# Edge sum of a two-layer graph network: a step's sum is added six steps behind its mark on VectorE instead of four

## The chip, the cores and the metric

The kernel runs on one core of a Trainium2 chip. The metric is the device time of one execution in microseconds (us); smaller is better. The kernel before takes 4176.44 us (median of three runs, 4168.92 to 4176.94).

## The reference

There are 12,500 nodes with 64 features each and 400,000 edges, sorted by their destination node. Every edge has a source, a destination and 64 attributes of its own. Two layers follow each other; cut to what matters:

```python
# layer 0
agg  = segment_sum(x[src], dst)
mean = agg / maximum(deg, 1)
h = relu(concat([x, mean]) @ W_fc + b_fc) + x @ W_res + b_res
x = layernorm(x + h)
# layer 1, two convolutions (the second on relu of the first)
msg = x[src] @ Wm + bm + edge_attr @ We + be
out = segment_sum(msg, dst) + x @ Ws + bs
x = layernorm(x + out)
```

Since `edge_attr @ We` is linear, its sum over the edges of a node is the sum of the edge attributes of that node, times `We`. The kernel therefore sums the attributes once, before either convolution needs them. This **edge sum** is the stage that the change touches: for each node, the sum of `edge_attr` over the edges that end in it.

## The kernel before, in words

The program has a preparing part (index tables, about 310 us), then three rounds of gathering and summing over the source nodes (`r` = 0, 1, 2), and between rounds 0 and 1 the edge sum. Each engine has a stream of its own, written out by hand, and streams meet at semaphores only. No scheduler orders anything: the order on each engine is the order of the code.

**A step of the edge sum.** The edges are cut into 625 groups of 640 (`EG` = 5 tiles of 128 edges). The nodes are cut into 98 blocks of 128. A step is one group with one block that its edges may end in; there are 728 steps (`ESTEPS`), which run in 91 passes of a loop with eight steps each (`EB` = 8). Which group and which block a step has is read from tables made earlier: `path` (groups) and `steps` (block numbers, one byte each, four to a word, lines 436 to 444). `h` is the step's place in the pass, 0 to 7, and also the number of its buffers: everything of a step lies in the `h`-th of eight slots, and its sum in PSUM bank `h`.

For each step:

- **SyncE (SP, lines 1498 to 1504)** loads the 160 KB of attributes of the group into `feats[h]`, once TensorE has finished with the slot (`e_mm[h]`). Before the first of the eight loads of a pass it reads eight group numbers from `path` into registers (line 431).
- **GpSimd (POOL, lines 1239 to 1248)** subtracts the first node of the block from the destinations of the group: `rel_e[h]`.
- **VectorE (DVE, line 878)** compares this with the numbers 0 to 127 and so makes the **mark** of the step, `mark_e[h]`: for each of the 640 edges a row of 128 places with a one at its node.
- **ScalarE (ACT, line 1373)** copies the marks of two steps at once from fp16 to fp32 (`hot_e`).
- **TensorE (PE, line 1130)** multiplies attributes and marks: five matrix products per step, recorded as ten, alternating between the two halves of the partitions of bank `h`. The last one raises `e_mm[h]`.
- **VectorE (line 889)** adds bank `h` to `sums_e` of the step's block: the **addition** of the step. It raises `e_add`, on which TensorE waits before it writes a bank again (line 1127).

**The order on VectorE** is what the change touches. In place `h` of the loop it makes the mark of step `h` and then the addition of the step that lies `LAG` = 4 behind (line 885: `b = (h - LAG) % EB`). In the first pass the first four additions add banks that were set to zero (line 871). After the loop four additions are left over (lines 890 to 895). Then TensorE folds the two halves together (lines 1135 to 1141), and round 1 begins.

```python
bs = load_blocks(i * (EB // 4) + (SETS * GW + GW - LAG) // 4, EB)
...
b = (h - LAG) % EB
dve.wait_ge(e_mm[b], i + (2 if h >= LAG else 1))
dve.wait_ge(e_add, i * EB + (h + EB))
to = flat(sums_e[:, bass.ds(bs[h], 1), :])
V.tensor_tensor(to, to, ps[:, b, 0:P], ALU.add).then_inc(e_add, 1)
```

Of the kernel before, what the change touches and what calls it, by code (L numbers as in the profile page):

```python
# [29 lines left out]
U8 = mybir.dt.uint8  # L30
# [5 lines left out]
P = 128  # L36
# [52 lines left out]
def gnn_program(nc, step_c, x, src, dst, edge_attr, W_fc, b_fc, W_res, b_res,  # L89
# [10 lines left out]
    D0, D1 = B0 * P, END * P  # L100
    REG, (RUNS, CSTEPS) = regions(), runs()
    BACK = max(k for _, _, _, k, _ in RUNS)
    CG = -(-CSTEPS // P)
    HIS = BLOCKS
    WIN = HIS * WD
    HALF = HIS // 2
    G, GW = 6, 8
    GI = WITH
    SG = -(-(T + BLOCKS - 1) // P)
    SPAD = SG * P  # L110
# [4 lines left out]
    EG = 5  # L115
    GROUPS = T // EG
    EB = 8
    LAG = 4
    ESTEPS = -(-(GROUPS + BLOCKS - 1) // EB) * EB
    ES = -(-(ESTEPS + 1) // P)  # L120
    NB = 7
# [8 lines left out]
    CH = 512 // VC  # L130
    CW = CG * P
    spans_of = [(s0, (REG + [(0, 0, 0, 0, CW)])[n + 1][4], wd) for n, (_, _, wd, _, s0) in enumerate(REG)]
    PIECES = 16
    HB, RING = 4, 16
# [6 lines left out]
    SETS = SPAD // G  # L141
    STEPS = SETS * GW + ES * P
# [4 lines left out]
    assert 3 * CG >= 64 and 4 * CG >= BLOCKS  # L147
    assert UNION >= YW >= BLOCKS * D and G * F1 <= 512 and 0 < GI <= ITERS and all(b <= 2 * GI or b - n >= 2 * GI for n, b in ((r[1], r[0] + r[1]) for r in REG)) and B0 >= 0 and DB % 2 == 0 and WPB % HB == 0
    assert all(n % 2 == 0 and s0 % P == 0 and sum(d) * WD // wd % RING == 0 for _, n, wd, ds, s0 in REG for d in ds) and HIS % 2 == 0 and (SETS - SETS % 2) * G >= T + BLOCKS - 1

    ctx = ExitStack()
    with ctx:
        def sb(name, shape, dt=F32):
            return ctx.enter_context(nc.sbuf_tensor(name, shape, dt))

        def sem(name):
            return ctx.enter_context(nc.semaphore(name))
# [13 lines left out]
        steps_dram = nc.dram_tensor("steps_dram", [SPAD + ES * P], U8).ap()  # L171
# [10 lines left out]
        code_g = sb("code_g", [P, SPAD], F16)  # L182
        src_g = sb("src_g", [P, SPAD], I16)
        path = sb("path", [1, PATH], I16)
        steps = sb("steps", [1, GW + STEPS], U8)
        base_e = sb("base_e", [P, ES * P])
        rel_e = sb("rel_e", [P, EB, EG, 2], F16)
        ident = sb("ident", [P, P])
# [68 lines left out]
        def c_ps(b):  # L257
            return ps[:, b, 0:CH * VC].rearrange("p (g v) -> p g v", v=VC)
# [54 lines left out]
        s_zero = sem("s_zero")  # L313
# [13 lines left out]
        s_path_in = sem("s_path_in")  # L327
# [108 lines left out]
        def load_blocks(frm, n):  # L436

            words = steps[0:1, :].bitcast(I32)
            _, packed = nc.values_load_multi_w_load_instructions(  # L439
                words[0:1, bass.ds(frm, n // 4)], engines=(ENG.DVE,), min_val=0,  # L440
                max_val=(BLOCKS - 1) * 0x01010101,
                skip_runtime_bounds_check_because="four block numbers, each clamped when the path was made")
            return [nc.s_assert_within(b, 0, BLOCKS - 1, skip_runtime_bounds_check_because="one of the four block numbers")
                    for v in packed for b in (v & 0x7F, (v >> 8) & 0x7F, (v >> 16) & 0x7F, v >> 24)]

        def flat(v):
            return v.rearrange("p b d -> p (b d)")
# [3 lines left out]
        def _(dve):  # L451
            V = nc.vector
            count = [0]

            def step(ins, name=None):

                count[0] += 1
                ins.then_inc(s_v, 1)
                dve.wait_ge(s_v, count[0])
                if name:  # L460
                    mark[name] = count[0]

            V.memset(steps[0:1, 0:GW + SETS * GW], 0).then_inc(s_zero, 1)
            V.memset(w_cat[:, :, :, :], 0.0).then_inc(s_zero, 1)
            V.memset(w_y0[:, :, :], 0.0).then_inc(s_zero, 1)
            dve.sem_inc(e_add, EB)
# [42 lines left out]
            for b in range(-(-CG // CH)):  # L509
                cols = slice(b * CH, min(b * CH + CH, CG))  # L510
                n = cols.stop - cols.start
                at, last = c_ps(b)[:, 0:n, :], found_c[:, 0:n, :]
# [174 lines left out]
            for r in range(3):  # L687
# [82 lines left out]
                if r == 0:  # L770
# [5 lines left out]
                    for b0, blocks, wd, deeps, s0 in REG:  # L776
                        upto, pair = steps_upto(wd, deeps)
                        many = at_once(wd)
                        with dve.Fori(0, blocks // 2) as i:
                            for j in range(2):  # L780
# [3 lines left out]
                                for q in range(upto[j][0], upto[j][WPB]):  # L784
# [12 lines left out]
                                    if part == 0:  # L797
                                        dve.wait_ge(b_used[j], it + (1 + j))
                                        if b0 < 2 * GI:
                                            bs = load_blocks((it * 2 + j) * (GW // 4), GW)  # L800
# [69 lines left out]

                step(V.memset(ps[:, EB - LAG:EB, 0:P], 0.0), "zeros_e")
                with dve.Fori(0, ESTEPS // EB) as i:
                    bs = load_blocks(i * (EB // 4) + (SETS * GW + GW - LAG) // 4, EB)
                    for h in range(EB):
                        if h % 2 == 0:
                            dve.wait_ge(e_hot[h // 2], i + 1)
                        dve.wait_ge(e_rel[h], i + 1)
                        marks = V.tensor_tensor(mark_e[:, h, :, :].rearrange("p j (c u) -> p j c u", u=2),  # L878
                                                lane16[:, 0:P].rearrange("p (c u) -> p c u", u=2).unsqueeze(1)
                                                .to_broadcast([P, EG, P // 2, 2]),  # L880
                                                rel_e[:, h, :, :].unsqueeze(2).to_broadcast([P, EG, P // 2, 2]),
                                                ALU.is_equal)
                        if h % 2:
                            marks.then_inc(e_mark[h // 2], 1)
                        b = (h - LAG) % EB
                        dve.wait_ge(e_mm[b], i + (2 if h >= LAG else 1))
                        dve.wait_ge(e_add, i * EB + (h + EB))
                        to = flat(sums_e[:, bass.ds(bs[h], 1), :])
                        V.tensor_tensor(to, to, ps[:, b, 0:P], ALU.add).then_inc(e_add, 1)  # L889
                last = load_blocks((SETS * GW + ESTEPS + GW - LAG) // 4, LAG)  # L890
                for k in range(LAG):
                    dve.wait_ge(e_mm[EB - LAG + k], ESTEPS // EB + 1)
                    dve.wait_ge(e_add, ESTEPS + k + EB)
# [491 lines left out]
        def _(sp):  # L1385
# [6 lines left out]
            row = lambda a: a.rearrange("(a n) -> a n", a=1)  # L1392
# [37 lines left out]
            for frm, to, cols in ((32, 0, ES), (56, PATH - P, 1)):  # L1430
# [4 lines left out]
            sp.dma_start(path[:, :], row(path_dram)).then_inc(s_path_in, 16)  # L1435
            sp.dma_start(steps[:, GW:GW + SETS * GW].rearrange("a (s e) -> a s e", e=GW)[:, :, 0:G],
                         row(steps_dram[0:SETS * G]).rearrange("a (s e) -> a s e", e=G)).then_inc(s_path_in, 16)
            sp.dma_start(steps[:, GW + SETS * GW:GW + STEPS], row(steps_dram[SPAD:SPAD + ES * P])).then_inc(s_path_in, 16)
            sp.dma_start(base_e[:, :], row(base_dram).to_broadcast([P, ES * P])).then_inc(s_path_in, 16)
            for r in range(3):  # L1440
                if r:
# [105 lines left out]
```

## Time and profile before

| what | before |
|---|---|
| median of three runs | 4176.44 us |
| lowest, highest | 4168.92, 4176.94 us |
| span of the profiled execution (first to last instruction) | 4128.3 us |
| mean granted TensorE clock over the span | 0.941 of full speed |
| PE busy over the span | 3373.4 us, 82% |
| VectorE, ScalarE, GpSimd busy | 57%, 40%, 48% |
| edge sum: first mark to last addition of the loop | 1594.9 to 2230.9 us |
| its last addition, after the loop | starts at 2234.21 us |
| fold of the halves on PE | 2234.55 to about 2256.5 us |

The times are read like this. A run's time is that of the whole execution; the span of the profiled execution is the part from its first to its last instruction, and 48.1 us lie between that span and the median of the runs. The profile gives no run time of its own for the profiled execution, so its span stands for it. The edge sum takes about 15% of the span, in one stretch, in which only the lines named above work. Register, semaphore and DMA-issuing instructions do not count as busy, so SyncE has no busy time at all in the profile; what it does shows in the starts of its DMAs and in the rows of its queue (SPq).

### The profile page before, as it was taken

Reading aid. Unit: us, or ns where it says so; the run is one execution under the profiler, and the core shown is the slowest. Engines: PE = TensorE matmul, PEld = TensorE weight load, DVE = VectorE, ACT = ScalarE, POOL = GpSimd, SP = SyncE. Lnnn points to the kernel's source line nnn. Section 1 sums busy time; section 2 is a strip of 40 time slices with the busy share of each in tenths; the row PEclk is TensorE's granted clock in tenths of the full one; section 3 lists DMA queues with packets and bytes.
Section 4 is the critical chain, followed back from the end, with each engine's and each line's share of the span. In section 5 each row is a group of like instructions: output and inputs, shape, how many; then the busy total and the mean of one; then the engine's idle time right before and its main releaser. Section 6 shows DMA issues by size and latency. Waiting matters only on the chain.

```text
span 4128.3 us, 116481 instructions
## 1 busy us (share of the span) xinstructions
PE 3373.4 (82%) x39555; PEld 3061.4 (74%) x39555; DVE 2361.8 (57%) x5334; ACT 1654.2 (40%) x2148; POOL 1962.3 (48%) x2298
## 2 busy tenths in 40 slices
PE   0148899999999995777778888899898789889894
PEld 0137888888888885666667778888888688888884
DVE  7579888898888885777775622222222322222224
ACT  0134577789999995777775400000000300000000
POOL 7722244456666662222221355555554655555552
PEclk9879999999999998999999689999999899999997
DMA  2542355556666664666664389888987798998984
GB/s 94 91 47 104 136 198 209 206 220 248 246 239 241 251 248 157 190 187 187 186 189 126 93 318 334 332 333 328 333 331 280 235 334 326 333 331 326 335 324 148
DMA packets 321181, 967.62 MB, mean 234 GB/s; under 512 B 145354, under 2 KB 238546, under 8 KB 262190
## 3 DMA queue, kind: packets, MB, share of 16 engines
q1 hardware_dynamic: 274338, 893.02, 60.9%
q0 software_dynamic: 46784, 73.84, 6.6%
q8 instruction: 34, 0.56, 0.1%
q14 instruction: 25, 0.20, 0.0%
HBM read 700.07 MB, written 269.81 MB: 235 GB/s over the span
## 4 chain that ended last, share of the span: by engine, by line
PE 64%; DVE 11%; issue 11%; POOL 4%; ACT 4%; DVEq 3%; DMA 2%; ACTq 0%; another core or an unknown queue 0%; POOLq 0%; SPq 0%
PE ps L1060 45%; PE ps L1083 11%; PE ps L1052 4%; DVE union L765 3%; DVE union L878 3%; ACT union L1373 3%; PE ps L1130 2%; DVE abuf L889 2%; POOL abuf L1170 1%; DVEq L439 1%; DVEq L889 1%; PE ps L1020 1%; POOL union L1170 1%; PE ps L974 1%; ACT abuf L1355 1%
## 5 line engine op out<-in xcount | busy, mean ns | idle before, releaser
L1223 POOL DMA_INDIRECT msg<-y_tab,idx x1368 | 1514.4, 1107 | 1373.2 <-ACT idx L1334 859.6
L1060 PE MATMUL ps<-union,abuf 128*128 128x192 bf16 x14896 | 1371.2, 254 | 90.5 <-issue 72.9
L1060 PEld LDWEIGHTS ps<-union,abuf 128*128 128x128 f16 x14896 | 1286.9, 101 | 147.6 <-issue 127.3
L1355 ACT ACTIVATE abuf<-ps 128x784 f16<-128x784 f32 x1216 | 998.6, 824 | 267.5 <-PE ps L1083 237.1
L765 DVE TENSOR_TENSOR union<-lane,union 128x1568 f16<-128x1568 f16 (+3 forms) x1440 | 950.4, 711 | 60.1 <-PE ps L1083 43.9
L1060 PE MATMUL ps<-early,abuf 128*128 128x195 bf16 x7546 | 857.0, 250 | 0.0
L1060 PEld LDWEIGHTS ps<-early,abuf 128*128 128x128 f16 x7546 | 680.0, 100 | 101.3
L1083 PE MATMUL ps<-union 128*128 128x392 f16 (+2 forms) x4288 | 694.1, 290 | 72.5 <-DVE union L765 46.0
L1334 ACT ACTIVATE idx<-src_g 128x6 int32 (+1 forms) x228 | 46.5, 205 | 1566.2 <-PE ps L1052 1035.9
L1130 PE MATMUL ps<-union 128*64 128x128 f32 x7280 | 479.9, 278 | 166.1 <-ACT union L1373 152.0
L1130 PEld LDWEIGHTS ps<-union 128*64 128x64 f32 x7280 | 394.3, 137 | 251.6 <-DVE abuf L889 184.7
L1373 ACT ACTIVATE union<-union 128x1280 f32<-128x1280 f16 x364 | 462.4, 1271 | 179.5 <-DVE union L878 172.5
L840 DVE TENSOR_REDUCE part_d<-ps 128x64 f32<-128x192 f32 x152 | 54.5, 358 | 699.3 <-PE ps L1060 490.0
L1083 PEld LDWEIGHTS ps<-union 128*128 128x128 f16 x4288 | 366.4, 109 | 111.3 <-ACT abuf L1355 46.9
L757 DVE TENSOR_TENSOR acc<-acc,ps 128x64 f32 (+1 forms) x918 | 203.7, 222 | 409.3 <-DVE acc L757 156.5
L1243 POOL TENSOR_TENSOR rel_e<-early,base_e 128x10 f16 x728 | 177.9, 264 | 474.5 <-DVE union L878 450.8
L878 DVE TENSOR_TENSOR union<-lane,rel_e 128x640 f16<-128x640 f16 x728 | 353.7, 486 | 67.4 <-issue 64.8
L889 DVE TENSOR_TENSOR abuf<-abuf,ps 128x128 f32 x728 | 206.2, 283 | 102.0 <-PE ps L1130 62.4
L1052 PE MATMUL ps<-msg,hot_g 128*128 128x64 bf16 (+1 forms) x4104 | 192.7, 197 | 84.4 <-issue 77.0
L746 DVE TENSOR_TENSOR hot_g<-code_g,lane 128x768 f16<-128x768 f16 x228 | 219.0, 960 | 74.3 <-DVE acc L757 55.8
L1052 PEld LDWEIGHTS ps<-msg,hot_g 128*128 128x128 f16 x4104 | 169.2, 100 | 97.7 <-issue 89.2
L974 PE MATMUL ps<-ident,abuf 128*128 128x128 f32 (+1 forms) x343 | 63.7, 346 | 82.8 <-DMA abuf<-x_pad 47.8
(230 smaller groups left out, 1329.0 us busy)
## 6 DMA issues: line engine op xcount, KB each, us to landing
abuf<-a_dram SPq DMA_DIRECT2D x304, 1568.0 KB
a_dram<-abuf SPq DMA_DIRECT2D x76, 3136.0 KB
union<-in_edge_attr_dram SPq DMA_DIRECT2D x728, 160.0 KB, 2.4
msg<-y_tab,idx POOLq DMA_INDIRECT x1368
y_tab<-union SPq DMA_DIRECT2D x28, 336.0 KB
y_tab<-early SPq DMA_DIRECT2D x7, 682.5 KB
abuf<-x_pad SPq DMA_DIRECT2D x7, 448.0 KB
abuf<-x_pad SPq DMA_DIRECT2D x14, 224.0 KB, 2.8
```

Of the source, the lines that this page charges most:

```text
L746: V.tensor_tensor(hot_g[:, j * G:(j + 1) * G, :], code_g[:, bass.ds((it * 2 + j) * G, G)].unsqueeze(2).to_broadcast([P, G, P]), lane16[:, ...
L757: V.tensor_tensor(to, to, tile_ps(r, j, k).unsqueeze(1), ALU.add).then_inc(s_add[r], 1)
L765: return V.tensor_tensor(to.rearrange("p s (c u) -> p s c u", u=2), lanes.unsqueeze(1).to_broadcast([P, n, width // 2, 2]), codes[:, which ...
L878: marks = V.tensor_tensor(mark_e[:, h, :, :].rearrange("p j (c u) -> p j c u", u=2), lane16[:, 0:P].rearrange("p (c u) -> p c u", u=2).uns ...
L889: V.tensor_tensor(to, to, ps[:, b, 0:P], ALU.add).then_inc(e_add, 1)
L1052: last = nc.tensor.matmul(tile_ps(r, j, k), hot_g[:, s, :], msg[:, s, c * width_of[r]:(c + 1) * width_of[r]], start=c == 0, stop=c == 2)
L1060: last = nc.tensor.matmul(ps[:, bank, 0:3 * width_of[r]], abuf[:, buffer, hi * P:(hi + 1) * P], ycols[r][:, hi, :], start=hi == 0, stop=hi ...
L1083: nc.tensor.matmul(ps[:, w % 4, 0:WIN].rearrange("p (h d) -> p h d", d=WD)[:, :, d0:d0 + wd], hot_c[:, n, WIN:WIN + P], hot_c[:, n, 0:HIS ...
L1130: last = nc.tensor.matmul(ps[half:half + D, h, 0:P], feats[:, h, j * D:(j + 1) * D], hot_e[:, h, j, :], start=j < 2, stop=j >= EG - 2)
L1223: pool.indirect_dma_start(msg[:, s, 0:3 * width_of[r]], None, y_tab[r], bass.IndirectOffsetOnAxis(ap=idx[:, s:s + 1], axis=0)).then_inc(ga ...
L1355: A.activation(abuf[:, j, :].rearrange("p (h w d) -> p w h d", w=WPB, d=WD) [:, w:w + 2, :, :], ps[:, w % 4:w % 4 + 2, 0:WIN].rearrange("p ...
L1373: A.activation(hot_e[:, h:h + 2, :, :], mark_e[:, h:h + 2, :, :], ACT.Copy)\
```

## The change

`LAG` goes from 4 to 6. Since a word of `steps` holds four block numbers, and 6 is not a multiple of four, the edge part of the table is stored two bytes later (`EDGE0`), so that the eight numbers of a pass again fill two whole words. With `LAG` = 6 the bank read in place `h` is `(h - 6) % 8`, six banks are set to zero ahead of the loop instead of four, six additions follow the loop instead of four, and their block numbers take two words instead of one. TensorE's wait at line 1127 has `LAG` in it and moves along.

```diff
-    LAG = 4
+    LAG = 6
+    EDGE0 = LAG % 4
...
-        steps = sb("steps", [1, GW + STEPS], U8)
+        steps = sb("steps", [1, GW + STEPS + 4], U8)
...
-            V.memset(steps[0:1, 0:GW + SETS * GW], 0).then_inc(s_zero, 1)
+            V.memset(steps[0:1, 0:GW + SETS * GW + EDGE0], 0).then_inc(s_zero, 1)
...
-                    bs = load_blocks(i * (EB // 4) + (SETS * GW + GW - LAG) // 4, EB)
+                    bs = load_blocks(i * (EB // 4) + (SETS * GW + GW + EDGE0 - LAG) // 4, EB)
...
-                last = load_blocks((SETS * GW + ESTEPS + GW - LAG) // 4, LAG)
+                last = load_blocks((SETS * GW + ESTEPS + GW + EDGE0 - LAG) // 4, EB)
...
-            sp.dma_start(steps[:, GW + SETS * GW:GW + STEPS], row(steps_dram[SPAD:SPAD + ES * P])).then_inc(s_path_in, 16)
+            sp.dma_start(steps[:, GW + SETS * GW + EDGE0:GW + STEPS + EDGE0], row(steps_dram[SPAD:SPAD + ES * P])).then_inc(s_path_in, 16)
```

On VectorE, in the middle of the loop, the addition that waits for bank 0 (the first step of the same pass, `e_mm0`) stands in the order before as follows (`union` is the mark, `abuf` holds `sums_e`, `e_rel4` is the fifth `rel_e`, `e_hot2` the third pair of ScalarE):

```order
L878 TENSOR_TENSOR union<-lane16,rel_e 128x640 [waits e_rel4,e_hot2]
L886 REGISTER_ALU
L887 REGISTER_ALU [waits e_mm0]
L889 REGISTER_ALU [waits e_add]
L889 ISA
L889 TENSOR_TENSOR abuf<-abuf,ps 128x128
L878 TENSOR_TENSOR union<-lane16,rel_e 128x640 [waits e_rel5]
L887 REGISTER_ALU [waits e_mm1]
```

and in the order of the change (lines are one further down):

```order
L879 TENSOR_TENSOR union<-lane16,rel_e 128x640 [waits e_rel6,e_hot3]
L887 REGISTER_ALU
L888 REGISTER_ALU [waits e_mm0]
L890 REGISTER_ALU [waits e_add]
L890 REGISTER_ALU
L890 ISA
L890 TENSOR_TENSOR abuf<-abuf,ps 128x128
L879 TENSOR_TENSOR union<-lane16,rel_e 128x640 [waits e_rel7]
L888 REGISTER_ALU [waits e_mm1]
```

The wait for bank 0 has moved from behind the mark of step 4 to behind the mark of step 6; the marks themselves stand as before.

On SyncE, the pass of the loads stands before as follows (the first rows of it and its end; six more pairs ISA and DMA lie between):

```order
L431 TENSOR_LOAD path
L1501 REGISTER_ALU
L1503 ISA [waits e_mm0]
L1503 DMA union<-in_edge_attr_64_dram 128x320
L1503 ISA [waits e_mm1]
```

and in the order of the change:

```order
L432 TENSOR_LOAD path
L1502 REGISTER_ALU
L1504 ISA [waits e_mm0]
L1504 DMA union<-in_edge_attr_64_dram 128x320
L1504 ISA [waits e_mm1]
```

Nothing has moved there but the line numbers: one read of `path`, then eight loads, each behind its wait.

## Rows read from the trace of the kernel before

**Rows 1.** Stretches of the edge sum: busy us (instructions) by engine, clock, DMA.
```profile
core 0: us, PE busy (x) PEld busy (x) DVE busy (x) ACT busy (x) POOL busy (x), PEclk, DMA share, GB/s
1592.00:1600.00 8.00, 2.43 (x24) 2.44 (x26) 3.74 (x12) 2.43 (x2) 2.91 (x12) 0.50 0.57 166
...
2000.00:2100.00 100.00, 74.97 (x1142) 61.50 (x1144) 73.72 (x230) 72.74 (x58) 27.76 (x114) 1.00 0.64 188
```
**Rows 2.** Timeline of VectorE, one pass: start us, us, line [idle before <-releaser].
```profile
1917.60 0.49 DVE L878 TENSOR_TENSOR union<-lane,rel_e 128x640 f16<-128x640 f16 x1 [0.72 <-issue]
1918.00 0.28 DVE L889 TENSOR_TENSOR abuf<-abuf,ps 128x128 f32 x1
1918.20 0.49 DVE L878 TENSOR_TENSOR union<-lane,rel_e 128x640 f16<-128x640 f16 x1
...
1919.48 0.29 DVE L889 TENSOR_TENSOR abuf<-abuf,ps 128x128 f32 x1 [0.19 <-issue]
...
1921.44 0.29 DVE L889 TENSOR_TENSOR abuf<-abuf,ps 128x128 f32 x1 [0.67 <-PE ps L1130]
...
1923.01 0.29 DVE L889 TENSOR_TENSOR abuf<-abuf,ps 128x128 f32 x1 [0.28 <-issue]
...
1923.62 0.28 DVE L889 TENSOR_TENSOR abuf<-abuf,ps 128x128 f32 x1
1924.61 0.49 DVE L878 TENSOR_TENSOR union<-lane,rel_e 128x640 f16<-128x640 f16 x1 [0.72 <-issue]
```
**Rows 3.** Timeline of ScalarE and TensorE, the same pass.
```profile
1918.86 2.62 ACT L1373 ACTIVATE union<-union 128x1280 f32<-128x1280 f16 x2 [0.87 <-DVE union L878]
1922.16 1.27 ACT L1373 ACTIVATE union<-union 128x1280 f32<-128x1280 f16 x1 [0.69 <-DVE union L878]
...
1918.22 1.31 PE L1130 MATMUL ps<-union 128*64 128x128 f32 x20 [0.22 <-ACT union L1373]
1920.26 1.31 PE L1130 MATMUL ps<-union 128*64 128x128 f32 x20 [0.73 <-ACT union L1373]
1921.76 1.31 PE L1130 MATMUL ps<-union 128*64 128x128 f32 x20 [0.18 <-DVE abuf L889]
1923.67 1.31 PE L1130 MATMUL ps<-union 128*64 128x128 f32 x20 [0.60 <-ACT union L1373]
```
**Rows 4.** Timeline of SyncE's queue: starts of the attribute loads around that pass.
```profile
1919.90 0.33 SPq L1503 DMA_DIRECT2D union<-in_edge_attr_dram  x1
1922.60 0.33 SPq L1503 DMA_DIRECT2D union<-in_edge_attr_dram  x1
...
1925.52 0.33 SPq L1503 DMA_DIRECT2D union<-in_edge_attr_dram  x1
1926.37 0.33 SPq L1503 DMA_DIRECT2D union<-in_edge_attr_dram  x1
1926.95 0.33 SPq L1503 DMA_DIRECT2D union<-in_edge_attr_dram  x1
1929.65 0.33 SPq L1503 DMA_DIRECT2D union<-in_edge_attr_dram  x1
```
**Rows 5.** SyncE's reads of `path`, line 431: duration ns min/median/max, first and last start.
```profile
L431 SPq TENSOR_LOAD <-path x90: 1651/1662/1688, 1597.7 to 2221.0; - x90
```
**Rows 6.** Waits of SyncE's queue in the edge sum: us in total, times, longest.
```profile
SPq L1502 <- PE ps L1130: 22.7, 94, 0.6
```
**Rows 7.** SyncE's queue near the start and the end of the edge sum.
```profile
1608.26 0.33 SPq L1503 DMA_DIRECT2D union<-in_edge_attr_dram  x1
...
2222.94 0.33 SPq L1503 DMA_DIRECT2D union<-in_edge_attr_dram  x1
...
2227.55 0.33 SPq L1503 DMA_DIRECT2D union<-in_edge_attr_dram  x1
```
**Rows 8.** DMA issues of the page: the attribute loads, us to landing.
```profile
union<-in_edge_attr_dram SPq DMA_DIRECT2D x728, 160.0 KB, 2.4
```
**Rows 9.** Timeline of the end of the edge sum: the last addition, the fold.
```profile
2234.21 0.29 DVE L895 TENSOR_TENSOR abuf<-abuf,ps 128x128 f32 x1 [0.26 <-DVE abuf L895]
...
2234.55 22.10 PE L1139 MATMUL ps<-twofold,abuf 128*128 128x64 f32 x196 [0.74 <-DVE abuf L895]
```
**Rows 10.** Timeline of the start: the zeroed banks, TensorE's first products.
```profile
1591.78 0.48 DVE L871 MEMSET ps<- 128x512 f32 x1 [1.12 <-issue]
...
1597.57 6.07 PE L1130 MATMUL ps<-union 128*64 128x128 f32 x60 [9.70 <-ACT union L1373]
...
1606.22 2.58 PE L1130 MATMUL ps<-union 128*64 128x128 f32 x40 [1.05 <-ACT union L1373]
```

## The prediction

> **What bounds the kernel now.** I read the stretches first, then one pass of the edge sum on each engine, then the queue of SyncE, and last the two ends of the stage.
>
> In the stretches of the edge sum [rows 1] TensorE, VectorE and ScalarE are each busy for 73 to 75 us of 100 and none is full, at a granted clock of 1.00 (2.4 GHz). The three wait for each other in a ring. The timeline of VectorE shows where [rows 2]. One pass of eight steps takes 1924.61 - 1917.60 = 7.0 us. Where nothing is waited for, an addition starts 0.40 us behind its mark (1917.60 to 1918.00) and the next mark 0.20 us behind the addition (1918.20), so a step costs VectorE 0.60 us. Four places of a pass cost more:
>
> - the third addition (place 2) is late by 0.28 (it would stand at 1919.20, it stands at 1919.48), the fifth (place 4) by 0.76 (1920.68 against 1921.44), the seventh (place 6) by 0.37 (1922.64 against 1923.01);
> - between the last addition and the first mark of the next pass lie 0.99 us instead of 0.20: the read of the block numbers and the branch, 0.79 more.
>
> The page calls two of the three late additions "issue", but all three start 1.18 to 1.26 us after TensorE began their products [rows 2, 3]: 1918.22 to 1919.48, 1920.26 to 1921.44, 1921.76 to 1923.01. They wait for products. And each product waits for ScalarE, which waits for the mark two places ahead. So the ring is: two marks, ScalarE (1.27 us), product (1.2 us until its addition may start), addition. Four places of VectorE are too short for it.
>
> The queue of SyncE is not counted as busy and is the row that matters most [rows 4]. It starts the first six loads of a pass 0.584 us apart (1922.60 to 1925.52, five gaps), the sixth gap is 0.85, the seventh 0.58, and from the last load to the first of the next pass it takes 2.70 us. In those 2.70 us lies a read of the group numbers of 1.66 us [rows 5], which it does not do ahead. In all passes together SyncE waits 22.7 us for TensorE [rows 6]. **Its own work fills nearly the whole pass:** 7 x 0.584 + 2.70 = 6.79 us of 6.98.
>
> **The change part by part.**
>
> *The additions two places later.* Take VectorE without any wait and count from the first mark of a pass. Mark h starts at 0.60h, its place's addition 0.40 later, the next pass begins at 8 x 0.60 + 0.79 = 5.59. ScalarE takes the first pair at 1.26 (as 1918.86 is to 1917.60) until 2.53, TensorE begins at 2.66, the first step can be added at 2.66 + 1.18 = 3.84. Place 4, where it stands now, comes at 2.80: a second too early. Place 6 comes at 4.00: in time. The second pair follows on ScalarE from 2.57 to 3.84, its products start behind those of the first pair at about 4.1 and can be added at 5.3, and the place for it is at 5.99. The third: ScalarE until 5.15, addition from 6.6, place 7.19. The fourth: ScalarE until 6.5, addition from 8.0, place 8.39. So the three late additions, 0.28 + 0.76 + 0.37 = 1.41 us a pass, go away as far as this ring is concerned, and it could run at 5.59 us.
>
> *What is late next.* A ring at 5.59 us asks SyncE for eight loads in 5.59 us, and it needs 6.79. TensorE must have the attributes, so the stage goes at SyncE's pace: 6.79. Does SyncE need TensorE in time for that? A load lands 2.4 us after its issue [rows 8], the products of the last step of a pass are done some 8 us after the first load of that pass was issued (2.4, eight steps of 0.66 and the end), and SyncE asks for them at 6.79 + 4.09 = 10.9. So the 0.2 us of waiting goes, and nothing comes in its place on SyncE. What shall remain on VectorE is a wait of 6.79 - 5.59 = 1.2 us a pass, at place 6, where the first products of the pass are added.
>
> *The sum.* From the third pass on the start is settled. Between the first loads of the third and the last pass lie 2222.94 - 1608.26 = 614.68 us for 88 passes, 6.985 each [rows 7]. At 6.788 these are 597.3 us: **-17.3**. The last pass has 4.61 us from first to last load; at SyncE's own pace it is 4.09: **-0.5**. Then the lead of the loads: now the last addition starts 2234.21 - 2227.55 = 6.7 us behind the last load [rows 7, 9], because loads wait long in their slots. When loads are late it is 2.4 for the landing, about 0.5 for the backlog on TensorE (eight steps of 0.66 against loads 0.584 apart), 1.2 for product to addition, 4.2 in all: **-2.5**. Together -20.3, I say **-20 us**. The fold begins behind the last addition and round 1 behind the fold [rows 9], with nothing beside them that has a time of its own, so all of it reaches the end.
>
> *Edits at nothing.* Zeroing six banks instead of four costs 0.24 us more by the 0.48 us of four [rows 10]. SyncE's first load does not wait for it, so it lies beside SyncE's start; without that cover it is 0.24. Two more additions in all (both of zeroed banks) are 2 x 0.60 = 1.2 us of VectorE, inside its 1.2 us of waiting per pass; uncovered, 1.2 once. The second word of block numbers behind the loop is read while the last products are awaited. The table stored two bytes later is one small transfer long before the stage. TensorE's wait for a free bank now asks for an addition that stands two places ahead of the step's own mark, which it waits for anyway: never last. No DMA is moved past another. GpSimd's rows have their marks as before.
>
> *A rule against a row.* SyncE's load rows stand 0.584 us apart even where no wait lies between, and 0.33 of that is the row of the load itself [rows 4]. The Trainium skill, page "Perfetto Trace Analysis", section "Identifying the Most-Contended Engine", says that the bottleneck is found by occupancy, the time an engine spends executing slices. Read so, SyncE is no candidate, VectorE's gaps are the thing to close, and the sum would be that of the second rival below.
>
> The forecast is thus 4128.3 - 20 = 4108 us of span, and with the 48 us between span and median 4156 us.
>
> **The rivals.**
>
> *Two: the full gain.* SyncE's 2.70 us could shrink when nothing holds it up, and the ring sets the pace: (6.985 - 5.6) x 91 = 126 us, 4050 us. For it speaks only that it does wait for TensorE now; against it that 2.70 stands in passes whose first load finds TensorE long done (load 1922.60, product of that slot from 1920.26), and that the waits of the stage sum to 22.7 us: SyncE cannot give more than that. A chance of 0.05.
>
> *Three: hardly anything.* SyncE's pass has only 0.2 us to lose. If its gaps grow by 0.1 us when loads and products fall closer together, under 8 us are left, 4168 us or more. Against it: gaps of 0.584 and 2.70 repeat to 0.01 us in passes far apart, and the DMA engines are at 0.64 [rows 1]. If the order on VectorE did not do what it says it would end here too, but the wait for bank 0 does stand behind the seventh mark. 0.10.
>
> *Four: slower, by the clock.* TensorE's idle time in a pass is now in four pieces, 0.22, 0.73, 0.18 and 0.60 [rows 3]. Once it waits for loads, they join into one gap of 6.79 - 8 x 0.66 = 1.5 us behind each burst. If that brings the granted clock to 1.2 GHz, as in the first stretch (0.50, after 9.7 us of idleness) [rows 1, 10], a step takes 6.07 / 6 = 1.0 us by the first sixty records and a pass 8.0: (8.0 - 6.985) x 91 = +92 us, 4269 us. It decides from about 6 of the 8 steps at the low clock. Against it: a gap of 1.05 us soon after the start [rows 10] was followed by records at the full clock. 0.05.
>
> **How the numbers follow.** The forecast has a chance of 0.80. Its own bounds are 17.8 us (the loads' pace alone) and 25 us (all 22.7 us of SyncE's waits and the 2.5 of the lead), with the 4 us by which runs of the kernel differ: 4147 to 4163. To take in part of the third case I draw the range from 4146 to 4168; outside lie the second and fourth case and half of the third. A measurement of this kernel tells about 0.2% (8.4 us) from no change. Faster: 0.78 of the forecast's 0.80 and 0.05 of the second, 0.83. Within 0.2%: 0.02 and 0.10, 0.12. Slower: 0.05.
>
> **What would show it.** In the profile after: passes of 6.79 us; first loads of successive passes 6.79 apart with all seven gaps at 0.584; SyncE's wait for TensorE near 2 us or less (only the start); VectorE's late additions gathered at place 6 as a wait of about 1.2 us for TensorE, 100 us in all, none at places 2 and 4; the last addition about 4.2 us behind the last load; the granted clock of the stage still 1.00; the fold starting near 2214. The prediction is wrong if passes are well under 6.7 us (SyncE is no bound), still 6.98 (something else than the ring held them), or if TensorE's clock falls.

## The result and the profile after

| what | before | after |
|---|---|---|
| median (six runs each) | 4168.04 us | 4141.93 us |
| lowest, highest | 4155.92, 4176.94 us | 4139.94, 4153.88 us |
| ratio, 95% interval | | 0.994 (0.9918 to 0.9961) |
| span of the profiled execution | 4128.3 us | 4139.6 us |
| time of the profiled execution | not given | 4141.38 us |
| first mark to last addition (rows below) | 1594.89 to 2234.21: 639.3 us | 1610.0 to 2228.24: 618.2 us |

The change makes the kernel 26 us faster by the medians; the interval of the ratio, applied to 4168 us, is 16 to 34 us. (Here and below the ratios leave out a few executions of 5234 to 14593 us, which occurred with the kernel before and with changed ones.) The edge sum itself is 21.1 us shorter. The span of the profiled execution is longer than before all the same: outside the edge sum it has 3521 us, the one before had 3489. That part of the program is the same in both kernels, and the section on the prediction comes back to it.

The timeline of VectorE, one pass of the change in the middle of the stage (start us, us, line, [idle before <-releaser]; it answers to [rows 2]):

```profile
1920.08 0.49 DVE L879 TENSOR_TENSOR union<-lane,rel_e 128x640 f16<-128x640 f16 x1 [0.72 <-issue]
1920.49 0.28 DVE L890 TENSOR_TENSOR abuf<-abuf,ps 128x128 f32 x1
...
1921.69 0.28 DVE L890 TENSOR_TENSOR abuf<-abuf,ps 128x128 f32 x1
...
1922.89 0.28 DVE L890 TENSOR_TENSOR abuf<-abuf,ps 128x128 f32 x1
...
1925.30 0.29 DVE L890 TENSOR_TENSOR abuf<-abuf,ps 128x128 f32 x1 [1.13 <-PE ps L1131]
...
1926.95 0.49 DVE L879 TENSOR_TENSOR union<-lane,rel_e 128x640 f16<-128x640 f16 x1 [0.77 <-issue]
```

The additions at places 2 and 4 (1921.69, 1922.89) follow without idle time. All the waiting stands at place 6, 1.13 us, in front of the first product of the pass.

The timeline of TensorE and ScalarE, the same pass (answers to [rows 3]):

```profile
1920.74 1.96 PE L1131 MATMUL ps<-union 128*64 128x128 f32 x30 [0.29 <-DMA union<-in_edge_attr_dram]
...
1921.34 3.59 ACT L1374 ACTIVATE union<-union 128x1280 f32<-128x1280 f16 x3 [0.87 <-DVE union L879]
...
1924.05 1.96 PE L1131 MATMUL ps<-union 128*64 128x128 f32 x30 [1.35 <-DMA union<-in_edge_attr_dram]
```

TensorE now waits for the landing of the attributes, a releaser that did not occur before. Over the whole stage the waits view of TensorE has two large entries (us in total, times, longest):

```profile
PE ps L1131 <- DVE abuf L890: 75.0, 69, 1.9
...
PE ps L1131 <- DMA union<-in_edge_attr_dram: 59.0, 77, 1.9
```

The larger one names VectorE's additions. By the order of the code they cannot be what came last: the addition that a product waits for stands two places ahead of the step's own mark on VectorE, and the product waits for ScalarE's copy of that mark as well. What ended these 75.0 us the view does not say; the experiments below show that they go away together with the waits for landings.

The starts of SyncE's loads (answers to [rows 4]): the last load of a pass, the whole next pass, and the first of the one behind it.

```profile
1918.84 0.33 SPq L1504 DMA_DIRECT2D union<-in_edge_attr_dram  x1
1921.53 0.33 SPq L1504 DMA_DIRECT2D union<-in_edge_attr_dram  x1
1922.12 0.33 SPq L1504 DMA_DIRECT2D union<-in_edge_attr_dram  x1
1922.70 0.33 SPq L1504 DMA_DIRECT2D union<-in_edge_attr_dram  x1
1923.28 0.33 SPq L1504 DMA_DIRECT2D union<-in_edge_attr_dram  x1
1923.86 0.33 SPq L1504 DMA_DIRECT2D union<-in_edge_attr_dram  x1
1924.45 0.33 SPq L1504 DMA_DIRECT2D union<-in_edge_attr_dram  x1
1925.03 0.33 SPq L1504 DMA_DIRECT2D union<-in_edge_attr_dram  x1
1925.61 0.33 SPq L1504 DMA_DIRECT2D union<-in_edge_attr_dram  x1
1928.31 0.33 SPq L1504 DMA_DIRECT2D union<-in_edge_attr_dram  x1
```

Seven gaps of 0.58 and then 2.70, pass after pass: SyncE waits for nothing. The waits in the stage, of SyncE's queue and of VectorE's additions, say the same (us in total, times, longest; the first answers to [rows 6]):

```profile
SPq L1503 <- PE ps L1131: 1.8, 4, 0.7
...
DVE abuf L890 <- PE ps L1131: 91.4, 94, 1.2
```

SyncE's read of the group numbers is as long as before ([rows 5]; ns min/median/max):

```profile
L432 SPq TENSOR_LOAD <-path x91: 1649/1658/1865, 1605.5 to 2218.0; - x91
```

The two ends of the stage in the timeline (answers to [rows 7] and [rows 9]): first load of the third and of the last pass, last load, last addition.

```profile
1623.12 0.33 SPq L1504 DMA_DIRECT2D union<-in_edge_attr_dram  x1
...
2219.92 0.33 SPq L1504 DMA_DIRECT2D union<-in_edge_attr_dram  x1
...
2224.00 0.33 SPq L1504 DMA_DIRECT2D union<-in_edge_attr_dram  x1
...
2228.24 0.29 DVE L896 TENSOR_TENSOR abuf<-abuf,ps 128x128 f32 x1 [0.36 <-PE ps L1131]
```

596.8 us for 88 passes are 6.78 each. The page of the profile says the same by its chain of work that ended last. SyncE's queue (SPq) had 0% of it before; the first line is the kernel before, the second the change, the third the change by line:

```profile
PE 64%; DVE 11%; issue 11%; POOL 4%; ACT 4%; DVEq 3%; DMA 2%; ACTq 0%; another core or an unknown queue 0%; POOLq 0%; SPq 0%
PE 62%; issue 12%; SPq 11%; DVE 6%; POOL 4%; DMA 2%; ACT 1%; DVEq 1%; another core or an unknown queue 0%; POOLq 0%; ACTq 0%
PE ps L1061 45%; PE ps L1084 11%; SPq L1504 7%; PE ps L1053 4%; SPq L432 4%; DVE union L766 3%; POOL abuf L1171 1%; PE ps L1021 1%; POOL union L1171 1%; PE ps L975 1%; PE ps L1140 1%; ACT abuf L1356 1%; DMA x_tab<-abuf 0%; POOL acc L1159 0%; DMA abuf<-x_tab 0%
```

Line 1504 holds the loads and line 432 the read of the group numbers.

A stretch in the middle of the stage (answers to [rows 1]; busy us by PE, PEld, DVE, ACT, POOL, then clock, DMA share, GB/s):

```profile
2000.00:2100.00 100.00, 77.36 (x1180) 67.43 (x1176) 73.90 (x238) 71.43 (x59) 33.18 (x118) 1.00 0.65 192
```

The clock stayed at 1.00 in this stretch, and on average from 1620 to 2210 us.

### The profile page after: what moved, and what is told of

It reads as the page before. It is cut to its first block, busy times and chain, and to the rows that moved or that the text cites. A ratio compares the mean times of both kernels' runs of the same rounds, so it can differ in the third digit from the quotient of the medians.

```text
span 4139.6 us, 116490 instructions
## 1 busy us (share of the span) xinstructions
PE 3379.6 (82%) x39555; PEld 3082.7 (74%) x39555; DVE 2347.3 (57%) x5336; ACT 1633.0 (39%) x2148; POOL 1999.5 (48%) x2298
## 4 chain that ended last, share of the span: by engine, by line
PE 62%; issue 12%; SPq 11%; DVE 6%; POOL 4%; DMA 2%; ACT 1%; DVEq 1%; another core or an unknown queue 0%; POOLq 0%; ACTq 0%
PE ps L1061 45%; PE ps L1084 11%; SPq L1504 7%; PE ps L1053 4%; SPq L432 4%; DVE union L766 3%; POOL abuf L1171 1%; PE ps L1021 1%; POOL union L1171 1%; PE ps L975 1%; PE ps L1140 1%; ACT abuf L1356 1%; DMA x_tab<-abuf 0%; POOL acc L1159 0%; DMA abuf<-x_tab 0%
## 5 line engine op out<-in xcount | busy, mean ns | idle before, releaser
L1131 PEld LDWEIGHTS ps<-union 128*64 128x64 f32 x7280 | 417.5, 137 | 207.6 <-DVE abuf L890 174.9
L1374 ACT ACTIVATE union<-union 128x1280 f32<-128x1280 f16 x364 | 442.4, 1263 | 178.1 <-DVE union L879 178.1
L1244 POOL TENSOR_TENSOR rel_e<-early,base_e 128x10 f16 x728 | 203.6, 301 | 427.8 <-DVE union L879 401.1
L890 DVE TENSOR_TENSOR abuf<-abuf,ps 128x128 f32 x728 | 204.9, 281 | 91.9 <-PE ps L1131 91.4
L815 DVE TENSOR_TENSOR acc<-acc,ps 128x65 f32 x456 | 99.9, 219 | 52.8 <-DVE acc L815 31.5
```

Of the source, the lines that this page charges most:

```text
L1131: last = nc.tensor.matmul(ps[half:half + D, h, 0:P], feats[:, h, j * D:(j + 1) * D], hot_e[:, h, j, :], start=j < 2, stop=j >= EG - 2)
L1374: A.activation(hot_e[:, h:h + 2, :, :], mark_e[:, h:h + 2, :, :], ACT.Copy)\
```

## The experiments

The theory: before, the ring of marks, ScalarE, products and additions sets the pace (6.98 us a pass); with six steps it could run at 5.6, but SyncE's own instructions take 6.79, so the change uncovers SyncE. The main rival: the 6.79 us come from elsewhere, for example the landing of the loads. The measure of every profile is the time from the first mark to the last addition, since it leaves out how long the rest of the program took. It comes from one profiled execution each; where a kernel was profiled twice, the two agree within 1.2 us.

### SyncE without its read of the group numbers, at four and at six steps

The same edit in the kernel before and in the change. It alters the computation: the attributes of group 6i + h are summed instead of those of the step's own group.

```diff
-                        grp = load(ENG.SP, i * EB, EB, GROUPS - 1)
...
-                            sp.dma_start(feats[:, h, :], ea[bass.ds(grp[h], 1), :, :].rearrange("g p c -> (g p) c"))\
+                            sp.dma_start(feats[:, h, :], ea[bass.ds(i * 6 + h, 1), :, :].rearrange("g p c -> (g p) c"))\
```

At four steps, expected:

> The kernel before (addition four steps behind), but SyncE takes the group number as 6i + h from its loop counter and does not read it from the table; so the attributes that are summed are those of other groups, at the same number and size of loads. Theory (the ring of mark, ScalarE, product and addition sets the pace before, SyncE has only 0.2 us of slack in a pass): the pass stays at 6.98 us, first load to last addition about 641 us, and SyncE waits for TensorE some 1.7 to 1.9 us more in every pass. Rival (SyncE was the bound before as well): the pass falls towards 5.6 us, the stage to about 515 us.

At six steps, expected:

> The change (addition six steps behind), with SyncE's read of the group numbers left out in the same way (group 6i + h, so other groups are summed). Theory (behind the change SyncE's own pass of 6.79 us is the bound, and the ring alone could run at 5.59): the pass falls to 5.6 to 5.7 us, first load to last addition to 515 us (510 to 525) from 620, the whole kernel by another 105 us below the change. Rival (the 6.79 us come from the landing of the loads or from the engines, not from SyncE's own instructions): the pass stays at 6.8.

At four steps the stage takes 1605.05 to 2244.38, 639.3 us, as before. The time that SyncE does not need for its read it waits. The waits of its queue at four steps:

```profile
SPq L1501 <- PE ps L1130: 186.1, 360, 1.0
```

and what VectorE's additions waited for, by the view of their line:

```profile
  PE ps L1130: 62.6, 92
  issue: 39.5, 178
```

SyncE's 186.1 us stand where [rows 6] has 22.7, and VectorE's 62.6 and 39.5 us are 62.4 and 39.4 in the kernel before. At six steps the stage takes 1611.0 to 2124.9, **513.9 us**, and the whole kernel 0.9713 (0.9661 to 0.9764) of the one before. In the whole stage VectorE's additions wait 0.5 us for products, once; what is left is the read of the block numbers. Two passes begin 5.61 us apart, and the addition at place 6 (1901.89) follows without idle time:

```profile
1897.88 0.49 DVE L879 TENSOR_TENSOR union<-lane,rel_e 128x640 f16<-128x640 f16 x1 [0.72 <-issue]
...
1901.89 0.28 DVE L890 TENSOR_TENSOR abuf<-abuf,ps 128x128 f32 x1
...
1903.49 0.49 DVE L879 TENSOR_TENSOR union<-lane,rel_e 128x640 f16<-128x640 f16 x1 [0.72 <-issue]
```

TensorE's waits for landings and for additions are both gone; it waits for ScalarE alone:

```profile
PE ps L1131 <- ACT union L1374: 71.8, 90, 9.4
```

In a stretch the DMA engines carry more (columns as above):

```profile
1700.00:1800.00 100.00, 87.40 (x1430) 76.74 (x1428) 87.10 (x286) 84.74 (x72) 40.57 (x144) 1.00 0.80 234
```

The same edit is worth nothing on one side and 104 us on the other. The distance on VectorE is worth 21 us with the read and 125 us without it. That is what two chains do of which only the longer one counts, and it shows that SyncE's instructions, not the landing of the loads, hold the change at 6.79: the loads are the same in number and size, and the DMA engines carry 234 GB/s here where they carried 192. The groups that are loaded are others, so these two runs alone leave open that such loads land sooner; the run with 32-bit values below, which loads what the change loads, closes that.

### A second read on SyncE, at four and at six steps

```diff
                         grp = load(ENG.SP, i * EB, EB, GROUPS - 1)
+                        again = load(ENG.SP, i * EB, EB, GROUPS - 1)
+                        grp = [(grp, again)[h % 2][h] for h in range(EB)]
```

> The change, with SyncE reading the eight group numbers twice in each pass (the second set is used for the odd steps, so everything is computed). Theory: SyncE's pass is the bound, so the whole second read is on the path: 6.79 + 1.66 = 8.45 us a pass, first mark to last addition 618 + 91 x 1.66 = 769 us (765 to 775). Rival (the wait of 1.2 us that VectorE has at place 6 gives room for a part of it): about 660.

> The kernel before (four steps behind), with the same second read on SyncE. Theory: SyncE's pass of 8.45 us lies above the ring's 6.98, so the stage is at SyncE's pace here too, 769 us from first mark to last addition (765 to 778), and the change of the distance from four to six is worth nothing against the run above (within 5 us). Rival (ring and SyncE's delays add up): 639 + 91 x 1.66 = 790.

At six steps 1591.45 to 2360.97, **769.5 us**; at four 1593.9 to 2365.1, **771.2 us**. The second read is wholly on the path of the change (151 us more than 618.2, 1.66 for each of the 91 passes), and with it the change of the distance is worth 1.7 us. The delays do not add up at four steps (790 would be that): the ring lies hidden behind SyncE. In the waits at four steps, TensorE waits for landings:

```profile
PE ps L1130 <- DMA union<-in_edge_attr_dram: 157.4, 85, 2.6
```

TensorE's clock, which the change left at 1.00, does fall here. At six steps with the second read:

```profile
1900.00:2000.00 100.00, 67.70 (x938) 62.79 (x938) 60.32 (x191) 58.93 (x48) 26.03 (x96) 0.90 0.51 153
2009.60:2010.40 0.80, 0.80 (x11) 0.80 (x8) 0.75 (x3) 0.30 (x1) 0.13 (x1) 0.50 0.95 319
```

The second line stands behind a gap of 2.79 us before the products that begin at 2008.13; about 1 us into them the granted clock is 0.50 (1.2 GHz) and stays so until about 2013. The stage is not longer for it: 769.5 us are what SyncE's own pass gives.

### Five steps

```diff
-    LAG = 6
+    LAG = 5
```

> The change with five steps instead of six. Place 4 without waits comes at 2.80 us, place 5 at 3.40, and the first product can be added at 3.84, so the ring has about 0.44 us of waiting at place 5 and somewhat more at the others: about 6.2 to 6.3 us a pass, below SyncE's 6.79. Theory: the stage is the same as with six, first load to last addition 620 to 622 us; VectorE's wait moves to place 5. Rival (the distance itself sets the gain): half way between 641 and 620.

1615.75 to 2233.11, 617.4 us: the same as six. VectorE's wait stands at place 5 now:

```profile
1916.62 0.29 DVE L890 TENSOR_TENSOR abuf<-abuf,ps 128x128 f32 x1 [1.09 <-PE ps L1131]
```

Timed six times, beside the kernel before:

> Five steps behind, timed in rounds. Its profile showed first mark to last addition 617.3 us, as the change has with 618.2 and 617.0. Theory: the same gain as six steps, 22 us by the stage, so a median 15 to 30 us below the kernel before. Rival (the sixth step matters outside the stage or in other executions): a clearly smaller gain, under 12 us.

The ratio is 0.9923 (0.9897 to 0.9949), median 4089.11 us against 4120.90 on the same chip; the profile gives 1595.5 to 2212.7, 617.2 us. As long as SyncE's pass takes 6.79 us, it is enough that the ring is quicker, however much.

### SyncE's read made cheaper

Four words of two group numbers each:

```diff
+            words = path[0:1, :].bitcast(I32)
+            _, packed = nc.values_load_multi_w_load_instructions(
+                words[0:1, bass.ds(frm, n // 2)], engines=(ENG.SP,), min_val=0, ...
+                    for v in packed for g in (v & 0x3FF, v >> 16)]
...
-                        grp = load(ENG.SP, i * EB, EB, GROUPS - 1)
+                        grp = load_pairs(i * (EB // 2), EB)
```

> The change, with SyncE reading the same eight group numbers as four words of two numbers each and taking them apart with register operations; everything is computed. Theory: a read of two words takes 0.53 us on VectorE's queue and one of eight values 1.66 on SyncE's, so four words about 0.9; less 0.75, plus about eight register operations of 0.03: a SyncE pass of about 6.3 us (6.1 to 6.4), first load to last addition about 575 us (560 to 585), the kernel about 45 us faster than the change. Rival (SyncE no bound): no change, 620 us.

> The kernel before (addition four steps behind), with SyncE's group numbers read as four words of two numbers; everything is computed. Theory (before, the ring and not SyncE sets the pace): nothing changes, first mark to last addition 639 us, SyncE waits for TensorE about 1 us in each pass. Rival (a shorter SyncE pass helps by itself): as much as behind the change, down to 543 us.

With six steps 1610.7 to 2153.6, **542.9 us**, and the kernel at 0.9764 (0.9705 to 0.9823) of the one before. The stage is some 32 us shorter than I expected, outside my 560 to 585. The read takes 0.31 us, not 0.9 (the row below), while the loads stand 0.62 and 0.67 us apart instead of 0.58, because the numbers are taken apart between them (in the run with 32-bit values, where nothing is taken apart, they stand 0.58 apart again): 5.95 us a pass.

```profile
L440 SPq TENSOR_LOAD <-path x91: 305/310/532, 1606.1 to 2144.3; - x91
```

With four steps 1594.4 to 2233.4, 639.0 us, as before, and SyncE waits 102.2 us for TensorE, 1.1 us a pass. Timed twelve times this is also the control for the whole kernel's time:

> Control for the whole kernel's time: four steps behind with the packed group numbers, whose profile showed the stage unchanged (639.0 us against 639.3). If the stage is all that counts, the median equals that of the kernel before within 8 us. If it differs by more, whole runs differ for a reason outside the stage, and the 26 and 30 us measured for the change can hold some of that.

The stage is again unchanged (1597.7 to 2237.1, 639.3 us), and the ratio is 0.9996 (0.9974 to 1.0018), which allows 11 us less or 7 more. But the medians, 4111.62 against 4120.90 us, differ by 9.3, more than the 8 that I had set. So with an unchanged stage a difference of up to 9 us between medians is to be expected here, and whole runs can't tell a surplus of some 5 us from nothing.

Why the read is so quick, the width of the values or their number, was not clear. Eight 32-bit values, copied once from the 16-bit table into a buffer that is free in this stage, decide between the two:

```diff
+        path_w = hot_g[:, :, :].rearrange("p s c -> p (s c)").bitcast(I32)[0:1, 0:ESTEPS]
...
+                dve.wait_ge(s_path_in, 64)
+                step(V.tensor_copy(path_w[:, :], path[:, 0:ESTEPS]), "path_w")
...
-                        grp = load(ENG.SP, i * EB, EB, GROUPS - 1)
+                        grp = load_wide(i * EB, EB)
```

> The change, with the group numbers copied once from 16-bit to 32-bit values before the stage, and SyncE reading eight 32-bit values in each pass, which it uses as they are; everything is computed. In the run with packed words the read of four 32-bit words took 0.31 us where eight 16-bit values took 1.65. Theory A (16-bit values are what is slow): eight 32-bit values take about 0.5 us, SyncE's pass is 6.79 - 1.15 = 5.65, level with the ring's 5.60; first mark to last addition 515 to 525 us, the kernel some 115 to 125 us below the kernel before. Theory B (each value costs about 0.2 us whatever its width, and the four packed words were quick for another reason): the read stays at 1.2 us or more, the pass at 6.3 or more, the stage at 575 us or more.

```profile
L440 SPq TENSOR_LOAD <-hot_g x91: 521/523/757, 1592.2 to 2104.4; - x91
```

Theory A holds: 0.52 us for eight values of 32 bits, against 1.65 for eight of 16 bits. The stage takes 1596.65 to 2113.83, **517.2 us**, and the kernel 0.9704 (0.9669 to 0.9739) of the one before, 3993.89 us against 4120.90 on the same chip. Its loads are those of the change, and they land no sooner (median 2.6 us against 2.5), so it is SyncE's own time that made the stage shorter. This kernel computes what the kernel before computes and is faster than both kernels of this study. It was not run at four steps; there the four packed words changed nothing.

### The change once more

> The change itself once more, with more rounds, to see how much of the whole kernel's difference is the stage's. Theory: the stage gives 21 us (first mark to last addition 618 against 639), and the rest of the kernel is the same on average though it differs by some 10 us between executions, so the median lies 15 to 27 us below the kernel before. Rival (the rest of the kernel gains too, for example by the clock): over 30 us.

0.9931 (0.9906 to 0.9955), 4093.17 us against 4122.83; the stage 1598.7 to 2215.7, 617.0 us. By the ratio 28 us (19 to 39), a little above the band I gave for the stage alone and just under that of the rival. The clock of the stage was not always 1.00 in this profile: behind a gap of 1.93 us (products that begin at 2080.94) it was 0.50 from 2082 to 2085, once between 2000 and 2100 us.

| steps behind | SyncE's read | first mark to last addition |
|---|---|---|
| 4 | eight 16-bit values (before) | 639.3 us |
| 4 | none | 639.3 |
| 4 | four packed words | 639.0, 639.3 |
| 4 | twice | 771.2 |
| 5 | eight 16-bit values | 617.4, 617.2 |
| 6 | eight 16-bit values (the change) | 618.2, 617.0 |
| 6 | twice | 769.5 |
| 6 | four packed words | 542.9 |
| 6 | eight 32-bit values | 517.2 |
| 6 | none | 513.9 |

## Why the prediction was right about the stage and wrong about the time

**The ring before.** That the three late additions are waits for products was right: with six steps none is left at places 2 and 4, and without SyncE's read none at place 6 either; the ring then runs at 5.61 us, where 5.59 was worked out. Against SyncE's 6.79 us five steps do as well; with a quicker read five were not run.

**What is late next.** Right, and shown from both sides: SyncE's own 6.79 us. Its wait for TensorE fell from 22.7 to 1.8 us, and VectorE's wait at place 6 is 1.13 us in the pass shown and 91.4 in all, where 1.2 and about 100 were expected.

**The sum.** 88 passes took 596.8 us, forecast 597.3. The last addition stands 2228.24 - 2224.00 = 4.2 us behind the last load, forecast 4.2 (whose terms 2.4, 0.5 and 1.2 add up to 4.1). The stage from first mark to last addition is 21.1 us shorter, forecast 20.3. The fold began near 2228.6 and not 2214 only because the whole stage began 15 us later in this execution.

**The step that failed** is the last one, from the stage to the time: "with the 48 us between span and median 4156 us". The 48 us were taken off the median to get the span and added again, so 4156 is the median of three runs, 4176.44, less 20. Two terms of it were mis-sized. The first is the level: three more runs of the kernel before (4167.16, 4164.07, 4155.92) brought its median to 4168.04, 8.4 us lower, where the prediction allowed 4 us for such differences. The second is the gain of the whole kernel: 26.1 us by the medians, where 20 were forecast. Together they are the 14.5 us between 4156.4 and 4141.93. Either alone would have stayed inside 4146 to 4168 (4148 or 4150); both together end 4 us below it. So the mechanism and the size of the stage's gain were right, and it was the range that was too narrow for a level known from three runs.

The 48 us are no time around the span either: in the profiled execution after, the time (4141.38) is 1.8 us above its span (4139.6), and so it is in every run since. The execution profiled before had a span 46 us shorter than that rule gives for 4176.44. Outside the edge sum it had 3489 us, the one after 3521; the twelve profiles taken after the first have between 3465 and 3549. Why the first was short stays open; the chip that it ran on is not on record. The kernel before had medians of 4166.2, 4122.83 and 4120.90 us on three chips in the later measurements, so the level alone moves by 45 us.

**The size of the whole gain** stays open by a few us. The stage gives 21 to 22 us. By the ratio, whole runs gave 25 and 28 for the change and 32 for five steps (16 to 34, 19 to 39, 21 to 42). All three lie above the stage's value, and each interval reaches down to it. Nothing shows that the surplus is real. The control with an unchanged stage had a median 9.3 us below the kernel before on the same chip; measured from that control instead, five steps are 22.5 us faster (4111.62 - 4089.11), which is what the stage gives. The version with 32-bit values has a stage 122 us shorter and is 0.0296 x 4121 = 122 us faster, with an interval of 108 to 136 that would also hold such a surplus. And on one chip the profiles leave for the rest of the program 3467 and 3479 us at four steps and 3474 and 3476 at six, so no difference. I can name no mechanism by which the rest of the program would gain some 5 us.

**The rivals.** The full gain did not come, but its number was good: 126 us were worked out, and 125 appear once SyncE is relieved. In the change the clock averaged 1.00 although TensorE's idle time gathered into one gap of some 1.4 us a pass beside shorter ones, so the fourth rival fell. What it describes does exist near by: the clock was 0.50 for some 4 us behind a gap of 1.93 us in the repeat of the change, and the stage averaged 0.90 with the second read, with a gap of 2.79 us in the lines shown. SyncE set the pace in both, and the stage was no longer for it (617.0 and 769.5 us). The third, hardly anything, fell too: gaps of 0.58 and 2.70 us did not move.

**The rule against the row.** By the rule of occupancy (the Trainium skill, page "Perfetto Trace Analysis", section "Identifying the Most-Contended Engine") VectorE's gaps were the thing to close. The runs side with the row: closing them gave a sixth of their worth (21 of 126 us), because a queue that the profile does not count as busy at all stood behind them.

## What to carry to other kernels

When a ring of engines is loosened, work out the pace of each queue that only issues, from the starts of its DMAs: it has no busy time in the profile, and as long as its own instructions take no less time, its total wait for the others is the most that the stage can gain. Here that bound was 22.7 us where the gaps of the ring promised 126. Behind the change a cheaper read on the queue was worth another 101 us, five times the change itself; ahead of the change, at four steps, the packed read was worth nothing. And a gain of 20 us is forecast as a ratio or difference on one chip; here the median moved by 8 us with three more runs and by 45 us between chips, and the span of one profile stood 46 us off.

## What was not expected of the hardware

The time to read registers from a table in SBUF depended strongly on the width of the values. SyncE took 1.65 us for eight 16-bit values (0.21 each), 0.52 us for eight 32-bit values and 0.31 us for four. GpSimd's reads of the same eight 16-bit values took 1.82 us (median), VectorE's reads of two 32-bit words 0.53. On SyncE the table of 16-bit numbers, read in each pass, was three times as dear as the same table in 32 bits.

The same work outside the edge sum took between 3465 and 3549 us in thirteen profiled executions, and mostly by the chip: 3525 to 3549 in four profiles on one, 3467 to 3479 in four on another, 3465 to 3473 in three on a third. Each chip was used at one time only, so chip and time are not told apart.
